# A two-block image kernel: statistics, projections and convolutions of the next image moved earlier, and the residual sum moved last in the chunk loop

## The chip, the cores and the metric

The kernel runs on one core of one Trainium2 chip. The metric is device time in microseconds (us), from the first to the last instruction of one launch, as the median of several runs. Engines: PE does matrix products, DVE (VectorE) and POOL (GpSimd) elementwise work, ACT (ScalarE) table functions and copies out of PSUM, SP issues the DMAs. Each works through its own list of instructions in order; semaphores tie them together.

## The reference, cut to what matters

`x` is (16, 192, 32, 32) in float32: 16 images of 192 channels and 1024 positions. Each image goes through two residual blocks, one after the other:

```python
def _L0_conv_ref(u, ...):                       # first block
    zxbcdt = useq @ in_proj_w.T                 # 192 -> 844 columns: z 384, xBC 448, dt 12
    dt = softplus(zxbcdt[..., -12:] + dt_bias)
    xBC = silu(depthwise_conv3x3(xBC) + conv_b) # over the 32x32 image
    x, Bm, Cm = split(xBC)                      # 384, 32, 32
    y = _chunk_scan(x, dt, A, Bm, Cm) + D * x   # 8 chunks of 128 positions, 12 heads
    y = layernorm(y) * norm_w + norm_b
    return (y * z) @ out_proj_w.T
def _L1_conv_ref(x, ...):                       # second block
    x_in, delta, Bm, Cm = split(seq @ W_proj.T + b_proj)
    delta = softplus(delta + dt_bias)
    y = _selective_scan(x_in, delta, A, Bm, Cm, D)   # 192 channels x 16 states, 1024 steps
    return y @ W_out.T + b_out
x = x + _L0_conv_ref(_gn(x), ...)               # _gn: 32 groups of 6 channels
x = x + _L1_conv_ref(_gn(x), ...)
```

## The kernel before

The work is a chain of passes. Pass b runs the second block's scan of image b beside the whole first block of image b+1; the first pass (b = -1) has no scan, the last two finish image 15. A pass is cut into 48 steps (`SLOTS`, the `s` in `run` of each engine), and every engine runs through the same steps in its own list. The order is fixed by hand, by a table of step numbers (`FILL_AT`, `CONV_AT`, `IM_AT`, `SSD_AT`, `P1_AT`) and by the order of the calls in each `run`. An engine that waits at one instruction holds up all that stands behind it in its list.

**The scan (image b).** One unit per step, 48 in all: ACT makes the decay factors (`decay`, L955), DVE multiplies the input (`inputs`, L1234) and runs the scan of the unit before (`scan_unit`, L1247), POOL multiplies by C (`states_by_c`, L754), and PE adds two units' states every second step (`sum_states`, the matmuls `bank<-hc,sel`). The unit's operands come by DMA from DRAM rows that the pass before wrote (`durep`, `bcrep`; `reads`, `keep`, `keep_rows`). The other half of `delta` gets its softplus on DVE in steps 1 and 2 (`softplus_piece`). Image b-1 gets its last output products in steps 10 to 13 (`finish`).

**The first block (image b+1).** In this order:
- step 0: channel statistics of the loaded image on DVE (`BATCH_NORM_STATS2 st<-xa`), step 1: their sums over groups on PE (`group_means`), step 2: `group_deviation` on DVE and `group_variances` on PE, step 3: `group_variance`, then POOL's power (`group_rstd`), step 4: the normalised image `xna`, `xnb` (`normalise_groups`, L1064 and L1065)
- steps 4 to 7: nine projection pieces on PE, "fills" (`fill`, `bank<-xna,wt0a`), copied by ACT one step later into `stage`, `bcst` and `dtx`
- steps 8 to 12: SP copies `stage` shifted by a pixel into `im` and `imb` (`shifted_copies`, 8 DMAs per convolution, L589)
- steps 8 to 11: four convolutions on PE (`conv`, `bank<-ssd,wcv`), three for x and one for B and C. ACT copies the three from PSUM into `xs` with the bias (`copy_conv`, L798), one step later
- steps 13 and 19: `silu` on ACT: Silu over both halves of `xs` (L892), and in step 13 over B and C from PSUM (L898). Each of the two loads the Silu table first and the exponential table afterwards
- steps 14 to 37: the chunk loop. Chunk c begins in step 14 + 2c; its parts stand 0 to 9 steps behind that (`chunk_at(s, stage)`). Two consecutive steps hold one part each of up to five chunks. In the second of the two steps DVE does, in order: the residual sum x1 = x + out of chunk c-4 (`residual`, L1125), the state carried on of chunk c-1 (`carry_state`, L1080 to L1083), the layer norm (L1112), the gate (L1119), and then the scan unit. PE's product `bank<-state,cs_` waits for the carried state
- from step 37 (`PRE_AT`): the statistics of x1, its `xna` at step 41, and the second block's eight projection tiles on PE (`project`, `bank<-xna,wt1a`): six at steps 41 to 47, the last two in steps 0 and 1 of the next pass. Then softplus and u for the first quarter (steps 43, 44), which SP writes to DRAM for the scan.

Program lines that the rows name: L798 `copy_conv`, L831 `exp_rows`, L892 `silu`, L1044 the channel statistics, L1053 to L1056 `group_deviation`, L1064 `normalise_groups`, L1082 `carry_state`, L1125 `residual`, L1234 `inputs`, L1284 PE's `mm`, used by nearly all products.

## Time and profile before

| | us |
|---|---|
| median of 3 runs | 4015.21 |
| lowest, highest | 3992.51, 4017.95 |
| profiled execution, its own time | 3989.59 |
| its span, first to last instruction | 3987.8 |

The profile is of one execution. A stretch of a pass is best read in the view of windows, which gives for each stretch the busy time of each engine and PE's granted clock as a share of full speed; the timeline then shows what an engine did there, and in brackets how long it had been idle and on what.

### The profile page before, as it was taken

What the parts mean: (1) busy time and instruction counts of PE and PEld (TensorE: products, weight loads), DVE (VectorE), ACT (ScalarE), POOL (GpSimd) and SP (SyncE); (2) the same over time, 40 slices, a digit from 0 to 9 for tenths busy, and PEclk for the clock granted to TensorE, in tenths of its full rate; (3) what the DMA queues carried; (4) which work ended last, traced back from release to release, by engine and by line L of the source; (5) the groups of instructions that cost most, each with busy time, mean ns of one, the idle gap of its engine ahead of it and who ended that gap; (6) DMA issues with size and microseconds to landing.
All of it is one profiled execution on the core that took longest, in us unless ns stands there. A gap on an engine that the chain in (4) does not pass through costs nothing. (4 is left out here: it accounts for less than half of the span.)

```text
span 3987.8 us, 62307 instructions
## 1 busy us (share of the span) xinstructions
PE 3274.6 (82%) x20256; PEld 1864.8 (47%) x20256; DVE 2674.3 (67%) x3855; ACT 1844.2 (46%) x4475; POOL 2035.9 (51%) x1363
## 2 busy tenths in 40 slices
PE   4778888887987978888887897978888888888875
PEld 2645446363453635436363463635536354463620
DVE  1346857678585776757678575775757668575798
ACT  1425454363544536444463534535454353544542
POOL 1325546364453745546365463745546364563755
PEclk8989989898998989989898998989989898998986
DMA  3032131312213132130422213132131312313122
GB/s 64 1 94 68 68 86 34 112 62 79 81 40 112 51 107 74 67 82 33 120 62 78 81 40 112 51 106 69 48 108 33 118 63 74 82 45 101 62 73 77
DMA packets 104179, 291.11 MB, mean 73 GB/s; under 512 B 25373, under 2 KB 27020, under 8 KB 103820
## 3 DMA queue, kind: packets, MB, share of 16 engines
q1 hardware_dynamic: 103820, 286.71, 23.8%
q8 instruction: 179, 2.93, 0.3%
q14 instruction: 180, 1.47, 0.1%
HBM read 181.84 MB, written 39.85 MB: 56 GB/s over the span
## 5 line engine op out<-in xcount | busy, mean ns | idle before, releaser
L754 POOL TENSOR_TENSOR hc<-hst,bcrep 128x512 f32<-128x512 f32 x768 | 1187.6, 1546 | 1227.8 <-DVE hst L1247 1199.8
L710 POOL TENSOR_TENSOR ssd<-ssd,cbt 128x512 f32<-128x512 f32 (+1 forms) x256 | 585.4, 2287 | 383.8 <-ACT ssd L831 364.2
L1234 DVE TENSOR_TENSOR wr<-durep,bcrep 128x512 f32<-128x512 f32 x768 | 644.4, 839 | 65.1 <-DMA bcrep<-bc_rows 65.1
L1284 PE MATMUL bank<-hc,sel 128*32 128x512 f32 x1536 | 474.6, 701 | 104.2 <-POOL hc L754 104.2
L955 ACT ACTIVATE bank<-durep,aneg 128x512 f32<-128x512 f32 x368 | 252.0, 690 | 514.0 <-DVE hst L1247 468.5
L831 ACT ACTIVATE ssd<-bank,ncs 128x128 f32<-128x128 f32 x1536 | 432.8, 401 | 74.6 <-PE bank L1284 72.5
L1284 PE MATMUL bank<-ssd 128*128 128x32 f32 (+1 forms) x3296 | 448.0, 288 | 7.4 <-POOL ssd L710 7.4
L1247 DVE TENSOR_TENSOR_SCAN hst<-dec,wr 128x512 f32<-128x512 f32 x256 | 358.2, 1399 | 135.6 <-ACT dec L955 63.0
L1284 PEld LDWEIGHTS bank<-ssd 128*128 128x128 f32 x3296 | 397.8, 193 | 15.1 <-POOL ssd L710 10.8
L1284 PE MATMUL bank<-xna,wt0a 128*128 128x128 f32 (+3 forms) x1088 | 320.1, 398 | 76.2 <-DVE xnb L1065 76.2
L861 ACT ACTIVATE ssd<-bank,nbc,nwc 128x128 f32<-128x128 f32 x384 | 147.8, 454 | 498.8 <-PE bank L1430 498.5
L1284 PE MATMUL bank<-ssd,wcv 64*32 64x512 f32 x5376 | 344.1, 591 | 0.0
L1247 DVE TENSOR_TENSOR_SCAN hst<-bank,carry,wr 128x512 f32<-128x512 f32 x240 | 306.9, 1279 | 29.4 <-issue 11.2
L955 ACT ACTIVATE dec<-durep,aneg 128x512 f32<-128x512 f32 x400 | 294.1, 740 | 7.1 <-DVE hst L1247 4.6
L1284 PE MATMUL bank<-xnb,wt0b 128*128 128x128 f32 (+3 forms) x1088 | 295.3, 374 | 0.0
L1284 PEld LDWEIGHTS bank<-xna,wt0a 128*128 128x128 f32 (+1 forms) x1088 | 183.1, 203 | 232.3 <-issue 195.5
L1368 PE MATMUL bank<-ident,csum 128*128 128x128 f32 x1536 | 257.3, 294 | 30.6 <-ACT ssd L831 30.6
L1368 PEld LDWEIGHTS bank<-ident,csum 128*128 128x128 f32 x1536 | 196.2, 149 | 89.4 <-ACT ssd L831 49.6
L1125 DVE TENSOR_TENSOR x1a<-bank,xa 128x128 f32<-128x128 f32 x128 | 37.1, 290 | 285.7 <-PE bank L1284 285.7
L1284 PEld LDWEIGHTS bank<-xnb,wt0b 128*128 128x128 f32 (+1 forms) x1088 | 178.7, 201 | 76.6 <-issue 76.6
L1247 DVE TENSOR_TENSOR_SCAN hst<-dec,carry,wr 128x512 f32<-128x512 f32 x144 | 209.2, 1453 | 6.9 <-issue 2.8
L1284 PE MATMUL bank<-ssd,wo 128*128 128x128 f32 (+1 forms) x1536 | 211.9, 280 | 1.2 <-DVE ssd L1119 1.0
(188 smaller groups left out, 5022.5 us busy)
## 6 DMA issues: line engine op xcount, KB each, us to landing
durep<-scratch SPq DMA_DIRECT2D x192, 512.0 KB, 3.8
bcrep<-bc_rows SPq DMA_DIRECT2D x128, 512.0 KB, 5.5
ssd<-stage SPq DMA_DIRECT2D x384, 140.4 KB, 2.9
ssd<-bcst SPq DMA_DIRECT2D x128, 74.4 KB, 2.1
xa<-in_x_dram SPq DMA_DIRECT2D x16, 512.0 KB, 5.3
scratch<-u SPq DMA_DIRECT2D x32, 256.0 KB, 2.0
scratch<-delta SPq DMA_DIRECT2D x32, 256.0 KB, 2.2
out_dram<-x1a SPq DMA_DIRECT2D x16, 512.0 KB, 5.1
```

Source lines behind the costliest of these rows:

```text
L710: nc.gpsimd.tensor_tensor(a, a, bc(cbt[:, c % 2, :].unsqueeze(1), [P, h1 - h0, Q]), ALU.mult).then_inc(att_ready.sem, 1)
L754: nc.gpsimd.tensor_tensor(hc[:, i % CRING, :], hst[:, i % HRING, :], bcrep[:, g, 1, :], ALU.mult).then_inc(hc_ready.sem, 1)
L831: ins = nc.scalar.activation(att[:, c % 2, h, :], bank[ROW_BANKS[r]][:, k * Q:(k + 1) * Q], ACT.Exp, bias=ncs[:, c, h:h + 1])
L861: ins = nc.scalar.activation(yzt[:, c % 2, m, :], bank[B_CBT][:, (m + 1) * Q:(m + 2) * Q], ACT.Identity, bias=nbc[:, m:m + 1], scale=nwc[: ...
L955: nc.scalar.activation(decay_of(i), durep[:, j % SLOTS_DU, 0, :], ACT.Exp, scale=aneg1[:, g * NB + k:g * NB + k + 1]).then_inc(decay_ready ...
L1125: nc.vector.tensor_tensor(x1a[par][:, t], bank[B_OUT][:, 0:Q], xa[:, t], ALU.add).then_inc(x1_ready.sem, 1)
L1234: nc.vector.tensor_tensor(wr[:, i % WRING, :], durep[:, j % SLOTS_DU, 1, :], bcrep[:, g, 0, :], ALU.mult).then_inc(w_made.sem, 1)
L1247: nc.vector.tensor_tensor_scan(hst[:, i % HRING, :], decay_of(i), wr[:, i % WRING, :], carry[:, g:g + 1] if hf else 0.0, ALU.mult, ALU.add ...
L1284: return nc.tensor.matmul(out, lhsT, rhs, start=start, stop=stop, skip_group_check=True)
L1368: nc.tensor.matmul(ps[:, k * Q:(k + 1) * Q], bc(csum[:, 0, c, h:h + 1], [P, P]), ident[:, :], start=(k == 0), stop=False, is_transpose=Tru ...
```

## The change

- **Statistics.** The statistics of image b+2 are taken in steps 42 to 46 of pass b (`EARLY_AT = 42`) instead of steps 0 to 3 of pass b+1; for image 0 they stand ahead of all passes. Their group sums go to bank 4, at other columns. `load_x` moves on SP from step 41 to step 38.
- **Projections.** `xna` is written in step 0, the fills stand in steps 0 to 2, their copies in steps 0 to 3. The chain of the step sizes dt moves with them, from steps 9 to 13 to steps 3 to 8.
- **Convolutions.** In the order x0, BC, x1, x2 at steps 3, 5, 7 and 10 instead of 8, 9, 10 and 11; the shifted copies at steps 2, 3, 4 and 7. `copy_conv` now puts each from PSUM through Silu with the bias and loads the exponential table again; `silu` is gone. `im` lies elsewhere in `ssd`, and the copies for x1 wait until the scan's softplus has left it.
- **Chunk loop.** It begins in step 13 instead of 14 (`SSD_AT`), with all that hangs on it. The residual sum stands last in its step on DVE, `layer_rstd` ahead of the second `attention` on POOL, and the exponentials of row block 1 ahead of the y copies on ACT.
- **Second block's projections.** All eight at steps 40 to 46 (`P1_AT`); none is left for the next pass.

The diff, cut to its core:

```diff
-FILL_AT = (4, 4, 5, 5, 6, 6, 6, 7, 7)
-CONV_ORDER = (0, 1, 3, 2)
-CONV_AT = (8, 9, 10, 11)
-IM_AT = (8, 9, 10, 12)
+FILL_AT = (0, 0, 1, 1, 1, 1, 2, 2, 2)
+FILL_COPY_AT = (0, 0, 1, 1, 2, 2, 2, 3, 3)
+CONV_ORDER = (0, 3, 1, 2)
+CONV_AT = (3, 5, 7, 10)
+IM_AT = (2, 3, 4, 7)
+IM_FILLS = (2, 6, 4, 9)
-SSD_AT = 14
+SSD_AT = 13
-P1_AT = (4, 4, 5, 8, 9, 10)
+P1_AT = (4, 4, 5, 7, 7, 8, 9, 10)
+EARLY_AT = 42
...
# SP, shifted_copies
+                sp.wait_ge(fill_copied.sem, fill_copied.at(n, IM_FILLS[u]))
+                if m == 1 and scan:
+                    sp.wait_ge(delta_ready.sem, delta_ready.at(n - 1, 3))
+                if m == 2:
+                    sp.wait_ge(conv_ps.sem, conv_ps.at(n, 1))
...
# ACT, copy_conv
+                for h in range(2):
+                    t = slice(h * HALF, (h + 1) * HALF)
+                    for q in range(2):
+                        if m < XM:
...
+                            ins = nc.scalar.activation(xs[m][r, t], bank[CONV_BANKS[u][q]][r0, :], ACT.Silu, bias=bias[r0, m:m + 1])
+                        else:
...
+                            ins = nc.scalar.activation((bs, cs_)[q][0:NS, t], bank[CONV_BANKS[u][h]][r, :], ACT.Silu,
+                                                       bias=cb[r, XM:XM + 1])
+                    ins.then_inc(conv_done.sem, 1)
+                nc.scalar.preload_act_table_set(EXP_LN)
...
# DVE, first_block_soon
-                if s == 4:
+                if s == 0:
                     if last:
                         dve.wait_ge(p1_ps.sem, p1_ps.at(n - 1, K_ALL))
                     normalise_groups(n, 0, xa[:, :], xb[:, :])
...
-                c = chunk_at(s, 9)
-                if c >= 0:
...
-                    residual(n, c, par)
...
# DVE, first_block_later (behind the scan unit and the inputs)
                 c = chunk_at(s, SSD_LAST)
+                if c >= 0:
...
+                    residual(n, c, par)
...
# DVE, run
+                    if more and s == EARLY_AT:
+                        loaded_stats(b + 2, early)
+                    if more and s == EARLY_AT + 2:
+                        group_deviation(b + 2, 0, early)
+                    if more and s == EARLY_AT + 3:
+                        group_variance(b + 2, 0)
...
# PE, start of the chunk loop
                     if c == 0:
-                        pe.wait_ge(silu_done.sem, silu_done.at(n, XM + 4))
                         pe.wait_ge(csum_ready.sem, csum_ready.at(n, 1))
-                        pe.wait_ge(conv_done.sem, conv_done.at(n, XM))
+                        pe.wait_ge(conv_done.sem, conv_done.at(n, 2 * len(CONV_ORDER)))
```

How the built program stands on the engines, at three places. PE, from the last steps of a pass into the next one (`mv` and `gq` are the image's statistics, `wt1a` and `wt1b` the second block's weights, `wt0a` the first block's). Before:

```order
L1284 MATMUL bank<-xna,wt1a 32x512
L1284 MATMUL bank<-xnb,wt1b 32x512
...
L1284 MATMUL bank<-mv,ga 128x1
...
L1284 MATMUL bank<-hc,sel 32x512 x2
...
L1284 MATMUL bank<-gq,ga 128x1
...
L1284 MATMUL bank<-xcm,diag1a 128x512
...
L1284 MATMUL bank<-hc,sel 32x512 x2
...
L1284 MATMUL bank<-xna,wt0a 128x512
```

And now:

```order
L1290 MATMUL bank<-mv,ga 128x1
...
L1290 MATMUL bank<-hc,sel 32x512 x2
L1290 MATMUL bank<-xna,wt1a 128x512
L1290 MATMUL bank<-xnb,wt1b 128x512
L1290 MATMUL bank<-gq,ga 128x1
...
L1290 MATMUL bank<-xna,wt1a 32x512
L1290 MATMUL bank<-xnb,wt1b 32x512
L414 UNCONDITIONAL_BRANCH
...
L1290 MATMUL bank<-hc,sel 32x512 x2
...
L1290 MATMUL bank<-xna,wt0a 128x512
```

The sums of the statistics now stand among the second block's projections, and a new pass (behind the branch) comes to its fills after one state sum.

ACT, around the last two convolutions (`dec<-durep` is the scan's decay). Before:

```order
L798 ACTIVATE xs<-bank,cb 64x512
L798 ACTIVATE xs<-bank,cbx 64x512 x2
L798 ACTIVATE xs<-bank,cb 64x512
...
L979 ACTIVATE x1b<-bank,boc 64x512
...
L892 ACT_TABLE_LOAD
L892 ACTIVATE xs<-xs 128x512 x3
...
L898 ACTIVATE bs<-bank,cb 32x512
L898 ACTIVATE cs_<-bank,cb 32x512
```

And now:

```order
L810 ACT_TABLE_LOAD
L810 ACTIVATE xs<-bank,cb 64x512
L810 ACTIVATE xs<-bank,cbx 64x512 x2
L810 ACTIVATE xs<-bank,cb 64x512
L816 ACT_TABLE_LOAD
...
L954 ACTIVATE dec<-durep,aneg 128x512
```

Each convolution has its own pair of table loads around its four instructions, and nothing of Silu is left behind the last one.

DVE, one step of the chunk loop. Before:

```order
L1125 TENSOR_TENSOR x1a<-bank,xa 128x128
L1126 TENSOR_TENSOR x1b<-bank,xb 64x128
L1082 TENSOR_TENSOR state<-state,cexp 32x384
L1083 TENSOR_TENSOR state<-state,bank 32x384
L1112 TENSOR_SCALAR ssd<-ssd,lmv,lrs 128x384
```

And now:

```order
L1079 TENSOR_TENSOR state<-state,cexp 32x384
L1080 TENSOR_TENSOR state<-state,bank 32x384
L1109 TENSOR_SCALAR ssd<-ssd,lmv,lrs 128x384
L1116 TENSOR_TENSOR ssd<-ssd,bank 128x384
L1241 SCALAR_TENSOR_TENSOR hst<-dec,carry,wr 128x512
L1228 TENSOR_TENSOR wr<-durep,bcrep 128x512
L1122 TENSOR_TENSOR x1a<-bank,xa 128x128
L1123 TENSOR_TENSOR x1b<-bank,xb 64x128
```

The carried state no longer stands behind the residual sum.

## Rows read from the trace of the kernel before

**Rows 1.** The page's part 1: busy us (share) and instructions per engine.

```profile
PE 3274.6 (82%) x20256; PEld 1864.8 (47%) x20256; DVE 2674.3 (67%) x3855; ACT 1844.2 (46%) x4475; POOL 2035.9 (51%) x1363
```

**Rows 2.** Windows of one pass: length; PE, PEld, DVE, ACT, POOL busy; PEclk, DMA, GB/s.

```profile
2411.90:2432.80 20.90, 9.35 (x26) 4.37 (x26) 19.85 (x30) 5.23 (x11) 7.94 (x6) 0.50 0.42 148
2432.80:2484.80 52.00, 51.90 (x452) 20.10 (x452) 21.81 (x30) 22.39 (x49) 14.46 (x9) 0.97 0.33 79
2484.80:2490.40 5.60, 0.07 (x3) 0.02 (x1) 3.29 (x4) 5.50 (x9) 3.17 (x2) 0.70 0.52 173
2490.40:2609.00 118.60, 106.02 (x701) 80.58 (x702) 90.20 (x136) 63.73 (x181) 80.15 (x53) 0.96 0.15 44
2609.00:2648.20 39.20, 33.86 (x86) 10.44 (x84) 32.14 (x44) 16.70 (x28) 20.41 (x14) 0.87 0.34 112
```

**Rows 3.** The instructions that write xna from the loaded image: durations in ns, first and last start in us.

```profile
L1064 DVE TENSOR_SCALAR xna<-xa,gm,gr x16: 812/1666/1668, 62.1 to 3628.8; 128x1024 f32<-128x1024 f32 x16
```

**Rows 4.** Timeline of PE, steps 1 to 4: start, us, instruction, [idle before <-releaser].

```profile
2415.30 0.59 PE L1284 MATMUL bank<-mv,ga 128*128 128x1 f32 x2 [6.51 <-DVE mv L1049]
...
2422.31 0.59 PE L1284 MATMUL bank<-gq,ga 128*128 128x1 f32 x2 [3.30 <-DVE gq L1056]
...
2432.84 2.04 PE L1284 MATMUL bank<-xna,wt0a 128*128 128x512 f32 x2 [4.90 <-DVE xnb L1065]
```

**Rows 5.** Timeline of PE, steps 8 to 14.

```profile
2451.67 1.05 PE L1284 MATMUL bank<-hc,sel 128*32 128x512 f32 x4
...
2452.97 5.38 PE L1284 MATMUL bank<-ssd,wcv 64*32 64x512 f32 x96
...
2466.06 5.36 PE L1284 MATMUL bank<-ssd,wcv 64*32 64x512 f32 x48
...
2490.39 0.79 PE L1284 MATMUL bank<-cs_,bs 128*128 128x128 f32 x2 [5.53 <-ACT cs_ L898]
```

**Rows 6.** Timeline of ACT, steps 9 to 13.

```profile
2459.15 1.38 ACT L798 ACTIVATE xs<-bank,cbx 64x512 f32<-64x512 f32 x2
...
2484.61 1.28 ACT L892 ACT_TABLE_LOAD   x1
2485.90 1.67 ACT L892 ACTIVATE xs<-xs 128x512 f32<-128x512 f32 x3
```

**Rows 7.** Timeline of PE, chunk loop, steps 23 to 25.

```profile
2552.55 0.91 PE L1284 MATMUL bank<-state,cs_ 128*128 128x384 f32 x2 [1.29 <-DVE state L1083]
...
2560.03 0.65 PE L1368 MATMUL bank<-ident,csum 128*128 128x128 f32 x4 [0.23 <-ACT ssd L831]
...
2566.20 0.91 PE L1284 MATMUL bank<-state,cs_ 128*128 128x384 f32 x2 [1.27 <-DVE state L1083]
```

**Rows 8.** Timeline of DVE, one step of the chunk loop.

```profile
2564.38 0.29 DVE L1125 TENSOR_TENSOR x1a<-bank,xa 128x128 f32<-128x128 f32 x1 [3.33 <-PE bank L1284]
...
2564.79 0.78 DVE L1082 TENSOR_TENSOR state<-state,cexp 32x384 f32<-32x384 f32 x1
```

**Rows 9.** Timeline of DVE, turn of the next pass.

```profile
2648.18 0.69 DVE L1234 TENSOR_TENSOR wr<-durep,bcrep 128x512 f32<-128x512 f32 x1 [3.16 <-DMA bcrep<-bc_rows]
2648.79 0.69 DVE L1044 BATCH_NORM_STATS2 st<-xa 128x6 f32<-128x512 f32 x1
...
2651.54 1.22 DVE L1247 TENSOR_TENSOR_SCAN hst<-bank,wr 128x512 f32<-128x512 f32 x1
...
2657.04 1.25 DVE L1054 TENSOR_TENSOR gd<-mv,gm 128x2 f32<-128x2 f32 x1
```

**Rows 10.** Timeline of SP, steps 8 and 9, and the copies' time to landing.

```profile
2438.65 11.45 SPq L589 DMA_DIRECT2D ssd<-stage  x16
...
DMA to landing us min/median/max: 2.3/2.9/4.1
```

**Rows 11.** Timeline of SP, last steps: u for the next scan goes to DRAM.

```profile
2637.99 0.34 SPq L521 DMA_DIRECT2D scratch<-u  x1
```

More of the change, by code:

```diff
@@ L755, in states_by_c, with run @@
                                         ALU.mult).then_inc(hc_ready.sem, 1)
-            def run(b, par, scan, end, first):
+            def run(b, par, scan, end, first, more):
                 for s in range(SLOTS if scan or first else 2):
@@ L767, in run @@
                         first_block(b + 1, s)
+                    if more and s == EARLY_AT + 4:
+                        group_rstd(b + 2, 0)
+            group_rstd(0, 0)
             passes(pool, run)
@@ L980, in finish, with run @@
                                          bias=boc[0:CB_, 1:2]).then_inc(out_ready.sem, 1)
-            def run(b, par, scan, end, first):
+            def run(b, par, scan, end, first, more):
                 step = Steps(act, act_steps, b + 1)
@@ L1248, in scan_unit, with run @@
                                              carry[:, g:g + 1] if hf else 0.0, ALU.mult, ALU.add).then_inc(scanned.sem, 1)
-            def run(b, par, scan, end, first):
+            early = Steps(dve, dve_early_steps, 0)
+            loaded_stats(0, early)
+            group_deviation(0, 0, early)
+            group_variance(0, 0)
+            def run(b, par, scan, end, first, more):
                 step = Steps(dve, dve_steps, b + 1)
+                early = Steps(dve, dve_early_steps, b + 2)
                 mid_step = Steps(dve, dve_mid_steps, b)
@@ L1579, in finish, with run @@
                     mm(o, wo1b[r, c], y1b[r, :], False, True).then_inc(o1_ps.sem, 1)
-            def run(b, par, scan, end, first):
+            def run(b, par, scan, end, first, more):
                 for s in range(SLOTS if scan or first else END_AT[1] + END_STEPS):
@@ L1618 @@
 PREPS = 15
-DVE_STEPS = 39
+DVE_STEPS = 35
+DVE_EARLY_STEPS = 4
 ACT_STEPS = 2
```

172 lines of the change are left out of this document (68 added, 104 removed).

## The prediction

> **What bounds the kernel now.** I began with the page's busy shares [rows 1]. No engine is full: PE is busy for 82% of the span, DVE for 67%. The bound must therefore change from stage to stage. The instruction that writes `xna` from a loaded image starts 16 times, first at 62.1 and last at 3628.8 us [rows 3]. One pass thus takes (3628.8 - 62.1) / 15 = 237.8 us. The windows cut one pass of 236.3 us into five stages [rows 2]:
>
> - Steps 0 to 4, 20.9 us: DVE is busy for 19.85, PE for 9.35 and only at half clock (1.2 of 2.4 GHz, share 0.50).
> - Fills and convolutions, 52.0 us: PE is busy for 51.9 of them, DVE for 21.8. PE bounds it.
> - Silu, 5.6 us: PE stands, ACT is busy for 5.5.
> - Chunk loop, 118.6 us: PE is busy for 106.0, DVE for 90.2.
> - Last steps, 39.2 us: PE busy for 33.9, DVE for 32.1. The scan units and softplus on DVE lead, PE follows closely.
>
> The timelines then name the gaps. In steps 1 to 4 PE waits three times for DVE's short statistics, 6.51, 3.30 and 4.90 us [rows 4]; behind the last comes the first fill. After the last convolution it waits 5.53 us for ACT's Silu [rows 5]. In the chunk loop it waits 1.27 us for the carried state and 0.23 us for ACT's exponentials in a chunk [rows 7]. The cause of the first stands on DVE [rows 8]: it sits 3.33 us in front of the residual sum, and the state (0.78 us and a second instruction) stands behind that in its list. PE had finished the state's product before.
>
> **The change, part by part.** All terms are per pass, against rows 2.
>
> *Steps 0 to 4.* The statistics leave, `xna` is written first. It takes 1.67 us [rows 3] and its `xnb` half of that: 2.5 us from its start to the first fill, in place of 20.9. The projections that PE did in these steps were already done while it waited. **-18.4 us.**
>
> *Fills and convolutions.* PE's work stays, and PE is full here. Added to the 52.0 us are what used to lie under the statistics: one state sum (1.05 us [rows 5]) and the product that opens the sum, 1.0 (half of the 2.04 of a pair of its size at half clock [rows 4]). The coupling is new: a convolution is 5.4 us of PE, the one for B and C too [rows 5]; ACT then needs two table loads of 1.28 and four instructions of 0.69 [rows 6], 5.35 us, and only behind them comes the decay for the next scan unit. That unit needs about 0.7 on ACT, 1.2 on DVE [rows 9] and 1.5 on POOL (the mean of all its instructions [rows 1]) before the sum on PE, so a state sum comes 9 to 10 us behind a convolution's end where it depends on it. It does so five steps behind the convolution. Between step 5 and step 10 PE has two sums, a small product and one convolution, 8.1 us, so it waits about 1.8 us. After step 3 it has over 13 us of other work, after step 7 over 12: hidden. The shifted copies take 11.45 / 16 = 0.72 us each to issue and 2.9 to land [rows 10], 8.6 us for the eight. Those for x0 can begin some 8 us after `xna`, and land at 17; the fills end at 21. The next eight land at 22 and 28, where PE wants them at 29 and 37. The DMAs stay hidden by 5 us or more. Together **+3.9 us**; bounds 0 (the coupling hidden) and +10 (each of the three earlier convolutions costs its 5.35 us of ACT, less what PE has to do meanwhile).
>
> *Silu.* The last convolution's copy is done 1.28 + 4 x 0.69 = 4.0 us after it. Before the chunk loop PE has in steps 11 to 13 five pairs of image b-1's output products of 1.0 us and a sum, over 6 us. They cover it. **-5.6 us**; if that cover were gone, 4.0 would come back.
>
> *Chunk loop.* With the residual sum last, DVE carries the state as soon as PE has made the product, over 2 us before PE asks for it. The wait of 1.27 goes in the four chunks in which a residual sum stands ahead, and that of 0.23 beside it with the new order on ACT: 4 x 1.5 = 6.0. A chunk now takes 2566.20 - 2552.55 = 13.7 us [rows 7], then 12.2, all of it PE's work; DVE is busy for 90.2 of 118.6 [rows 2], 10.4 of the 13.7. PE is late next, so no other engine takes the wait over. At the loop's start the pause for Silu is gone. The stage has a clock share of 0.96, so 0.08 of 118.6 us, 9.5, are at half clock, in which up to 4.7 are lost. The pause before it left the clock at 0.70. I take 3.5. The sums that DVE waits for in the last chunks cost up to 3.3 each [rows 8], mostly beside PE's own work: 2. One more state sum falls into the stage: +1.05. **-10.5 us**, bounds -4 (the state alone, little of it) and -14.
>
> *Last steps.* DVE gets four statistics instructions of 0.6 to 0.7 and the rest of them, 2.8 us, and the deviation (with one instruction of 1.25) 1.9 [rows 9]. A step more lies here, 1.22 + 0.69 [rows 9] = 1.9. Off goes the wait of 3.16 us for `bcrep` [rows 9]: from SP's first store of `u` [rows 11] to the end of that wait it is 10.2 us, and 13 us of steps and `xna` now cover it. The scan unit of 1.2 comes behind `xna`. The eight projections are now all ahead of `xna`. From the deviation on PE has its group sum, two projections and a state sum, about 6.0 us at full clock and 12 at half; DVE has three steps, 6.0. I take 2 of the 0 to 6. `load_x` is issued three steps earlier and has more than 10 us. **+4.2 us**, bounds +2 and +10.
>
> A pass: -18.4 + 3.9 - 5.6 - 10.5 + 4.2 = **-26.4 us**, 236.3 to 209.9. PE would be busy for over 90% of it. There are 15 such turns: 396 us. Image 0's first block, which runs without a scan, loses its own wait for Silu and those for the state, about 12. From the profiled execution's 3989.6 us: 3989.6 - 396 - 12 = 3582. That execution lies at the lower edge of the three timed runs, 0.6% below their median, so I round up to **3585**.
>
> A rule that speaks against this change is in the Trainium skill, "ScalarE: Activation LUTs", section "What ACT_TABLE_LOAD costs": every switch of tables costs a load of about 1.28 us and a drain of nearly 1.4 behind it, so functions should be grouped by table. This case's trace agrees with the load alone: the instruction behind it starts 1.29 us after the load's start [rows 6], so no drain shows. By the page's 2.66 us a convolution's copies would take 8.1 us instead of 5.35, and the sum would be some 4 us per pass less gain, 3645.
>
> **The rivals.**
>
> *The loads cost about double when they stand between matmuls' copies* (chance 0.07). Against it are the two loads of the row at 1.28 and their neighbours without a gap. Each copy would take 2 x 1.28 longer, of which PE has cover for the outer ones: 4.2 us per pass, 3582 + 63 = 3645.
>
> *ACT paces the convolutions* (0.14). For it: PE, ACT, DVE and POOL hand each scan unit on in order, and eight loads and 16 Silu instructions stand in eleven steps. If each of the three earlier convolutions costs PE 4 us of waiting, where I have 1.8 in all, and the last steps give back their upper bound (6 more), the gain is 26.4 - 10.2 - 4 = 12 us per pass: 3989.6 - 180 - 12 = 3798, and 3700 for half of it.
>
> *More than I count* (0.04): the clock stays up everywhere, the chunk loop reaches its bound: 32 us per pass, 3498.
>
> *No change* (0.02): the stages are only shifted, because a resource that I take as covered (the shifted copies, the scan's durations beside POOL) has no room: 3990.
>
> *Slower, through PE's clock in the last steps* (0.03). In steps 42 to 46 PE now waits for DVE between narrow group sums, the pattern before which it ran at 0.50 in steps 0 to 4 [rows 2, 4]. If it fell there and stayed, the 33.9 us of PE in this stage at share 0.87 would become 59, where DVE has 43.4: `xna` would be 15.6 us late, and the fills (18.8 us from 2432.84 to 2451.67 [rows 4, 5]) would take 16 more. That is 31.6 us against the 26.4 gained, +5.2 x 15: 4068. It decides once both together exceed 26.4 us. Against it: in the last steps the clock share was 0.87 with such group sums among them, and five of the eight projections keep PE busy around them.
>
> **The numbers.** The forecast has 0.70, with 3500 to 3690 from its bounds taken half together. The range must add the part of the coupling rival that lies below 3740 and the loads: **3490 to 3740** leaves out 0.17. A measurement of this kernel tells about 1% from no change. Faster by over 1%: all but the last two cases, **0.95**; within 1% **0.02**, slower **0.03**.
>
> **What would show it.** In the profile after: passes of about 210 us between the starts of `xna`; no PE wait on `mv` or `gq` above 2 us ahead of the fills and a first fill 2.5 us after `xna` starts; PE above 0.9 busy from there to the chunk loop; no PE wait for the Silu outputs; the wait on `state` gone for the later chunks; a chunk at 12.2 us; DVE's wait for `bcrep` gone; ACT_TABLE_LOAD at 1.28 with its neighbour at once behind it. It would be wrong if PE waits for POOL's `hc` by more than 3 us in steps 8 to 12, or if DVE waits for the eighth projection ahead of `xna` by more than 6.

## The result, and the profile after

The changed kernel takes 3692.76 us (median of 4 runs, 3677.62 to 3702.86), beside 4003.86 us for the kernel before on the same chip: a ratio of 0.9218, 95% interval 0.9163 to 0.9274. 3585 us had been forecast, in a range of 3490 to 3740. The gain is 311 us where about 420 were expected. The profile after is of the slowest of the four runs (3702.86 us) and the profile before of an execution below all its timed ones (3989.59 us). Two executions of the changed kernel differ by up to 25 us, 1.7 us a pass, so a stage's difference of that size between two profiles needn't come from the edit.

The page's part 1, busy times by engine, answers to [rows 1]:

```profile
PE 3197.5 (86%) x20256; PEld 1857.6 (50%) x20256; DVE 2943.3 (80%) x3855; ACT 1863.1 (50%) x4443; POOL 2115.8 (57%) x1363
```

The first surprise is here. VectorE (DVE) has the same 3855 instructions as before, and 269 us more of busy time. The instruction that opens a pass, with its shortest, median and longest duration in ns and its first and last start, answers to [rows 3]:

```profile
L1061 DVE TENSOR_SCALAR xna<-xa,gm,gr x16: 811/814/1420, 62.2 to 3346.2; 128x1024 f32<-128x1024 f32 x16
```

A pass takes (3346.2 - 62.2) / 15 = 218.9 us, for 237.8 before: 18.9 less, where 26.4 were forecast. The windows of one pass (busy PE, PEld, DVE, ACT, POOL, then PE's granted clock) answer to [rows 2]. They are: `xna` to the first fill, fills and convolutions, the way to the first `b_by_c`, the chunk loop, the last steps.

```profile
1573.40:1575.30 1.90, 0.00 (x0) 0.00 (x0) 1.90 (x3) 1.87 (x4) 0.52 (x1) 1.00 0.85 298
1575.30:1629.10 53.80, 51.06 (x445) 21.22 (x445) 33.58 (x42) 34.24 (x61) 20.18 (x13) 0.90 0.52 136
1629.10:1635.30 6.20, 6.14 (x19) 1.28 (x15) 4.02 (x5) 5.96 (x10) 3.25 (x2) 1.00 0.00 0
1635.30:1753.20 117.90, 104.24 (x706) 80.82 (x706) 111.65 (x141) 58.95 (x178) 88.28 (x55) 0.97 0.16 52
1753.20:1794.00 40.80, 32.91 (x102) 11.36 (x100) 34.93 (x54) 15.12 (x25) 18.69 (x14) 0.92 0.34 113
```

The chunk loop is as long as it was (117.9 for 118.6 us), but DVE is busy for 111.7 of it, where it was 90.2. Everywhere else the pass went much as planned. Means over the 14 passes from the second to the last but one, read from the starts of the named instructions, in us:

| stage | before | after | difference | forecast |
|---|---|---|---|---|
| last residual sum to the next pass's first fill | 61.03 | 43.64 | -17.4 | -18.4 + 4.2 = -14.2 |
| first fill to the end of the last convolution | 48.41 | 52.81 | +4.4 | +3.9 |
| from there to the first `b_by_c` | 11.17 | 5.93 | -5.2 | -5.6 |
| chunk loop | 118.85 | 119.28 | **+0.4** | **-10.5** |
| pass | 239.46 | 221.65 | -17.8 | -26.4 |

Inside the loop, the starts of PE's state products after the first `b_by_c` show where the chunks stand, again as means over these passes (the first chunk has none, so product 2 is the third chunk's):

| kernel | 1 | 2 | 3 | 4 | 5 | 6 | 7 |
|---|---|---|---|---|---|---|---|
| before | 10.3 | 22.3 | 34.2 | 47.9 | 61.5 | 75.2 | 89.0 |
| after | 9.4 | 21.9 | **37.6** | 50.3 | 63.0 | 75.8 | 89.2 |

The second product comes 0.4 us earlier and the third 3.4 us later, and the four that follow win only 3.2 us back. Product to product, they take 12.7 to 12.8 us (the last 13.4) where 12.2 were forecast and 13.7 measured before. So two things need a cause: the late third product, and the chunk of 12.7 to 12.8.

The timeline of DVE at the second product (start, duration, instruction):

```profile
1653.03 0.66 DVE L1228 TENSOR_TENSOR wr<-durep,bcrep 128x512 f32<-128x512 f32 x1
1653.61 2.69 DVE L1079 TENSOR_TENSOR state<-state,cexp 32x384 f32<-32x384 f32 x1
1656.34 0.54 DVE L1080 TENSOR_TENSOR state<-state,bank 32x384 f32<-32x384 f32 x1
```

The same on GpSimd (POOL), whose spans are rough:

```profile
1653.42 2.48 POOL L719 TENSOR_TENSOR ssd<-ssd,cbt 128x1024 f32<-128x1024 f32 x1
1655.85 1.58 POOL L761 TENSOR_TENSOR hc<-hst,bcrep 128x512 f32<-128x512 f32 x1
```

And on PE:

```profile
1652.08 1.05 PE L1290 MATMUL bank<-hc,sel 128*32 128x512 f32 x4
1657.03 0.94 PE L1290 MATMUL bank<-state,cs_ 128*128 128x384 f32 x2 [3.89 <-DVE state L1080]
```

The decay of the state is a product of 32x384 elements whose shortest length in this trace is 0.60 us. It began 0.2 us behind POOL's 2.48 us product and ended some 0.4 us behind its end: 2.69 us. PE stood for 3.89 us. Then its clock fell, as the two windows around the wait show:

```profile
1653.00:1657.00 4.00, 0.14 (x2) 0.00 (x1) 3.97 (x5) 1.75 (x5) 4.00 (x3) 1.00 0.03 11
1657.00:1661.00 4.00, 3.97 (x17) 3.51 (x18) 4.00 (x4) 1.14 (x4) 4.00 (x4) 0.59 0.02 4
```

PE is idle for 3.9 us of the first window, and in the second the granted clock is 0.59, mostly at the lower of its two levels (1.2 of 2.4 GHz). PE's work now runs right up to the loop, so the half-clock stretch that stood at its start before is gone, but another opens behind the second product. In the first 45 us of the loop PE is at half clock for 8.1 us of a pass before and for 9.0 after (means over the 14 passes, from the trace's records of the clock).

In the later chunks PE has another wait. Its timeline shows this one in a chunk of the changed kernel:

```profile
1703.21 0.46 PE L1290 MATMUL bank<-cs_,bs 128*128 128x128 f32 x2 [0.69 <-ACT ssd L880]
```

L880 is ACT's copy of the transposed output. Before the change, a state sum of the scan (`bank<-hc,sel`, 1.05 us) stood between the transposition and this `b_by_c` and covered the copy. The scan's sums stay in the even steps, and the loop now starts in an odd one, so the sum has come to stand ahead of the state product, and nothing covers the copy. From the third product to the seventh PE waits 2.74 us for this copy, 0.69 a chunk, and 0.49 for the state; before the change it was 5.01 for the state, 0.69 for the exponentials and nothing for the copy. These are the groups of the `b_by_c` over a whole run (count | busy, mean ns | idle before it, by what ended it), in the kernel before with the residual sum moved (kernel 1 below) and in the changed kernel:

```profile
L1283 PE MATMUL bank<-cs_,bs 128*128 128x128 f32 x256 | 68.1, 351 | 94.6 <-ACT cs_ L898 91.2 <-ACT ssd L861 3.4
L1290 PE MATMUL bank<-cs_,bs 128*128 128x128 f32 x256 | 57.5, 307 | 49.3 <-ACT ssd L880 44.5 <-ACT xs L810 4.7
```

The 91.2 us are the wait for Silu at the loop's start. L861 is the same copy in kernel 1: 3.4 us in a whole run, for 44.5.

DVE is nearly full in these chunks, busy for 48.4 of 51.6 us. Its timeline in one of them:

```profile
1704.53 2.78 DVE L1228 TENSOR_TENSOR wr<-durep,bcrep 128x512 f32<-128x512 f32 x1
1707.23 1.61 DVE L1079 TENSOR_TENSOR state<-state,cexp 32x384 f32<-32x384 f32 x1
```

Beside it on POOL:

```profile
1704.18 2.58 POOL L719 TENSOR_TENSOR ssd<-ssd,cbt 128x1024 f32<-128x1024 f32 x1 [0.43 <-ACT ssd L847]
1706.72 1.72 POOL L761 TENSOR_TENSOR hc<-hst,bcrep 128x512 f32<-128x512 f32 x1
```

`wr`, 0.66 us a moment ago, takes 2.78 behind the large product, and the state product then meets `hc`. The groups of the profile sort DVE's instructions in this kernel into two kinds. These work on SBUF alone and can stretch beside POOL: `wr` 0.65 to 2.79 us, the state product 0.60 to 2.71, the normalisation 0.46 to 2.52, the scan 1.20 to 2.92. The 128x384 products with an operand in PSUM stay at 0.53 to 0.56 us whether POOL works or not, the scans with one at 1.22 to 1.28, and `bn_stats`, with its one input, at 0.56. The Trainium skill, "SBUF — State Buffer", section "Who interferes with whom", states a rule for this: a VectorE instruction with two inputs in SBUF, beside a GpSimd one that reads SBUF, or one in a mode that uses both of VectorE's pairs of ports, needs a pair that GpSimd uses too; the pair is a lock for a whole instruction, and the one that is issued second stands. The trace agrees with its form: the state product ended 0.4 us behind POOL's, and wasn't slowed in proportion. Whether the normalisation, with one tensor in SBUF as input, runs in such a mode, no run here shows.

### The profile page after: what moved, and what is told of

The parts are those of the page before. It is cut to its first block and busy times, and to the rows that moved or that the text cites. A ratio compares the mean times of both kernels' runs of the same rounds, so it can differ in the third digit from the quotient of the medians.

```text
span 3701.1 us, 61373 instructions
## 1 busy us (share of the span) xinstructions
PE 3197.5 (86%) x20256; PEld 1857.6 (50%) x20256; DVE 2943.3 (80%) x3855; ACT 1863.1 (50%) x4443; POOL 2115.8 (57%) x1363
## 5 line engine op out<-in xcount | busy, mean ns | idle before, releaser
L761 POOL TENSOR_TENSOR hc<-hst,bcrep 128x512 f32<-128x512 f32 x768 | 1252.3, 1631 | 977.1 <-DVE hst L1241 938.7
L1228 DVE TENSOR_TENSOR wr<-durep,bcrep 128x512 f32<-128x512 f32 x768 | 769.6, 1002 | 1.4 <-DMA bcrep<-bc_rows 1.4
L1290 PE MATMUL bank<-hc,sel 128*32 128x512 f32 x1536 | 444.3, 663 | 122.5 <-POOL hc L761 120.7
L1241 DVE TENSOR_TENSOR_SCAN hst<-dec,wr 128x512 f32<-128x512 f32 x256 | 443.0, 1731 | 94.0 <-ACT carry L995 62.9
L1290 PE MATMUL bank<-ssd 128*128 128x32 f32 (+1 forms) x3296 | 467.4, 296 | 0.6 <-POOL ssd L719 0.4
L1290 PEld LDWEIGHTS bank<-ssd 128*128 128x128 f32 x3296 | 419.6, 202 | 5.6 <-POOL ssd L719 1.4
L1290 PE MATMUL bank<-xna,wt0a 128*128 128x128 f32 (+3 forms) x1088 | 305.8, 384 | 38.1 <-DVE xnb L1062 38.1
L880 ACT ACTIVATE ssd<-bank,nbc,nwc 128x128 f32<-128x128 f32 x384 | 147.5, 453 | 355.2 <-PE bank L1436 355.2
L1241 DVE TENSOR_TENSOR_SCAN hst<-bank,carry,wr 128x512 f32<-128x512 f32 x240 | 306.2, 1276 | 13.4 <-ACT bank L954 4.4
L1374 PE MATMUL bank<-ident,csum 128*128 128x128 f32 x1536 | 242.5, 282 | 11.5 <-ACT ssd L847 10.7
L724 POOL TENSOR_TENSOR lrs<-lve,neghalf 128x1 f32<-128x1 f32 x128 | 97.9, 765 | 241.2 <-DVE lve L1105 241.2
L1290 PEld LDWEIGHTS bank<-hc,sel 128*32 128x32 f32 x1536 | 58.8, 112 | 322.2 <-POOL hc L761 214.0
```

Source lines behind the costliest of these rows:

```text
L724: nc.gpsimd.tensor_tensor(lrs[:, c % 2:c % 2 + 1], lve[:, c % 2:c % 2 + 1], neghalf[:, 0:1], ALU.pow).then_inc(lrs_ready.sem, 1)
L761: nc.gpsimd.tensor_tensor(hc[:, i % CRING, :], hst[:, i % HRING, :], bcrep[:, g, 1, :], ALU.mult).then_inc(hc_ready.sem, 1)
L880: ins = nc.scalar.activation(yzt[:, c % 2, m, :], bank[B_CBT][:, (m + 1) * Q:(m + 2) * Q], ACT.Identity, bias=nbc[:, m:m + 1], scale=nwc[: ...
L1228: nc.vector.tensor_tensor(wr[:, i % WRING, :], durep[:, j % SLOTS_DU, 1, :], bcrep[:, g, 0, :], ALU.mult).then_inc(w_made.sem, 1)
L1241: nc.vector.tensor_tensor_scan(hst[:, i % HRING, :], decay_of(i), wr[:, i % WRING, :], carry[:, g:g + 1] if hf else 0.0, ALU.mult, ALU.add ...
L1290: return nc.tensor.matmul(out, lhsT, rhs, start=start, stop=stop, skip_group_check=True)
```

## The experiments

I went in with three theories for the missing 10.9 us of the chunk loop. **A**: DVE's idle time, once taken away, turns into longer instructions beside POOL. **B**: DVE comes late out of the convolutions. **C**: ACT's new order sets the chunk. **D**, that the odd first step of the loop makes the chunk longer, came with the seventh kernel. The ratios are to the kernel before, timed beside each, with 95% intervals.

**1. The residual sum last, and nothing else.** The four lines move from `first_block_soon` of the kernel before to its `first_block_later`:

```
-                c = chunk_at(s, 9)
-                if c >= 0:
-                    ...
-                    residual(n, c, par)
...
             def first_block_later(n, s, step, par, again):
...
                 c = chunk_at(s, SSD_LAST)
+                if c >= 0:
+                    ...
+                    residual(n, c, par)
```

> The kernel before, with one part of the change: the residual sum of a chunk is the last of its step on VectorE instead of the first; nothing else is moved. The prediction's working (residual out of the way, a chunk at the floor of the matrix work, 12.2 us) takes some 6 us off each of 15 passes: 4004 - 90 = 3915 us. Theory A (VectorE's and GpSimd's products slow one another down, so that VectorE's idle time in front of the residual turns into longer instructions of VectorE): chunks of 12.8 for 13.7 us at most, 3 to 4 us a pass, 3945 us, with the product wr going from 0.92 us to 1.2 or more in the chunk loop. Theory C (ScalarE's order sets the chunk): no change, 3990 to 4010 us.

Measured: 3900.48 us, ratio 0.9735 (0.9705 to 0.9765). From the third product to the seventh a chunk takes 12.1 to 12.6 us, the forecast's 12.2. So the step of the forecast was right for the kernel before, and theory A's 12.8 was wrong for it, though POOL's hold is there too: DVE is busy for 46.8 of the 49.2 us from the third product to the seventh, as full as after the change. DVE in a later chunk of this kernel:

```profile
1803.19 0.67 DVE L1233 TENSOR_TENSOR wr<-durep,bcrep 128x512 f32<-128x512 f32 x1
1803.88 2.61 DVE L1082 TENSOR_TENSOR state<-state,cexp 32x384 f32<-32x384 f32 x1
```

And POOL:

```profile
1803.39 2.69 POOL L710 TENSOR_TENSOR ssd<-ssd,cbt 128x1024 f32<-128x1024 f32 x1 [2.79 <-ACT ssd L831]
```

Here `wr` starts 0.2 us ahead of the product and escapes it; after the change it starts 0.35 us behind it and does not. One long stall a chunk here, a long and a middling one there. Neither makes PE wait long for the state: 0.39 us a chunk here, 0.16 there (the table behind kernel 9).

**2. The changed kernel with the residual sum first again** (the same lines moved back).

> The changed kernel with one part undone: the residual sum is again the first of its step on VectorE. Prediction's working and theory A: the idle time in front of the residual comes back (about 16 us over three chunks before), and the chunk goes from 12.8 to about 13.7 us: 3.6 us a pass, 3745 us. If the residual's place is worth nothing because VectorE and GpSimd share their work's time anyway, 3693 us, and wr falls back from 1.5 to 0.9 us in the later chunks.

Measured: 3709.80 us, ratio 0.9258 (0.9236 to 0.9280). The interval overlaps that of the whole change, and the medians' ratios differ by 0.4%. So the parts don't add up: alone, the residual's place is worth 2.7%. These are the groups of the residual's first instruction over a whole run, with DVE's idle time ahead of it. Before:

```profile
L1125 DVE TENSOR_TENSOR x1a<-bank,xa 128x128 f32<-128x128 f32 x128 | 37.1, 290 | 285.7 <-PE bank L1284 285.7
```

This experiment:

```profile
L1122 DVE TENSOR_TENSOR x1a<-bank,xa 128x128 f32<-128x128 f32 x128 | 36.8, 287 | 78.9 <-PE bank L1291 78.9
```

With the residual first, DVE still waits only 78.9 us for it, not 285.7: another edit had taken most of this wait away as well. And a chunk takes 12.7 to 12.8 us either way, with DVE busy for 44.8 us of four chunks instead of 48.4 and PE's 0.69 us for the copy as it was. What sets 12.8 is thus neither the residual nor a full DVE. My forecast of 13.7 failed here, and so did that of a short `wr` (its mean is 1.00 us in both kernels).

**3. ACT's copy of the scan's carry ahead of the convolutions' copies** (theory B).

```
 second_half(b, s, par, mid_step)
+if 2 <= s < HU + 2:
+    ...
+    nc.scalar.copy(carry[:, s - 2:s - 1], ...).then_inc(carried.sem, 1)
 ...
 first_block(b + 1, s, step, 1 - par, scan, end)
-if 2 <= s < HU + 2:
-    ...
```

> The changed kernel, with ScalarE's copy of the scan's carry put ahead of the first block's work in its step, so that it no longer stands behind the copy of a convolution (VectorE idles 5.00 and 2.37 us for it in the two steps before the chunk loop). Theory B (the loop loses its gain at its start, because VectorE comes late out of the convolutions): VectorE's 5.00 us wait goes, the state of the third chunk is there in time, its 3.9 us wait and the half-clock stretch behind it go; 4 to 5 us a pass, 3625 us. Theory A alone: VectorE starts two scans earlier, but its instructions stay stretched beside GpSimd's; 1 to 2 us a pass, 3670 us. If neither, 3693 us.

Measured: 3725.72 us, ratio 0.9318 (0.9289 to 0.9347), slower by 1.1%. DVE began the second product's decay of the state only 0.2 us earlier after the first `b_by_c`, and found the same POOL product in its way: 2.69 us again. So this edit hardly moved DVE and by itself says little on B. Kernel 8 below does: DVE begins the same decay no earlier there (18.7 us after the first `b_by_c`, for 18.5), and the loss is gone. B is out. The time is lost after the loop: from the last residual sum to the next first fill it takes 46.2 us for 43.6, with PE at half clock for 20.2 us of it for 13.2. Why was not tried.

**4 to 6. The two small orders undone.** In kernel 4 the copy of the transposed output stands ahead of the exponentials of the second row group again, in kernel 6 POOL's rstd behind its second attention product, in kernel 5 both.

```
 # ScalarE (4 and 5)
-c = chunk_at(s, 2)
-if c >= 0:
-    exp_rows(n, c, 1)
 c = chunk_at(s, 6)
 ...
+    exp_rows(n, c, 1)
     exp_rows(n, c, 2)
 # GpSimd (5 and 6)
-c = chunk_at(s, 4)
-if c >= 0:
-    layer_rstd(n, c)
 ...
     attention(n, c, HPB, NH)
+c = chunk_at(s, 4)
+if c >= 0:
+    layer_rstd(n, c)
```

In the expectation of kernel 4 I have this order the wrong way round: the edit puts the copy ahead of the exponentials, not behind them.

> The changed kernel with ScalarE's order undone: the copy of the transposed output stands behind the exponentials of the second row group again. Theory C (this order makes TensorE wait for the copy, 0.68 us a chunk, and so sets the 12.8 us): the wait changes and the pass with it; with the copy behind the exponentials (1.1 us) it should be there later and the wait should grow by about 1 us a chunk, some 5 us a pass, 3765 us. Theory A: TensorE is not the bound in the chunk loop, 3693 us within 15.

> The changed kernel with both small orders of the chunk loop undone: ScalarE's copy of the transposed output stands ahead of both later groups of exponentials again, GpSimd's rstd of the layer norm behind the second attention product again. Theory A, now in this form: a two-operand product, state product or normalisation of VectorE that lies in SBUF alone stands still while a GpSimd instruction runs (wr 2.79 us beside the 2.44 us product, 0.67 us free), so that the period of a chunk hangs on which VectorE instruction each GpSimd instruction meets. With the old orders GpSimd's 1024-wide product starts after wr, as in the kernel before with the residual last, and the chunk falls from 12.8 toward 12.2 us: 4 us a pass, 3635 us. If the two orders matter only through ScalarE's own time, 3732 us as with ScalarE's order alone undone. If the place of the chunk loop in the steps decides, 3693 us.

> The changed kernel with GpSimd's rstd of the layer norm behind the second attention product again, ScalarE's order as changed. Theory A: rstd comes 2.5 us later, so VectorE's normalisation waits for it, but wr may run before the product: between 3665 and 3720 us; the trace must show fewer long wr and the lost time as a wait for rstd or a longer state product. The rival that the chunk loop is bound by rstd's chain alone (stats, rstd, normalisation, transposition): 2.5 us a chunk, over 3900 us.

Measured: 4, 3732.33 us, ratio 0.9318 (0.9299 to 0.9336); 5, 3748.09, 0.9390 (0.9357 to 0.9423); 6, 3708.63, 0.9269 (0.9215 to 0.9322). Undoing ACT's order costs about 1%, 13.3 us a chunk for 12.8: the new order is worth keeping, and C, by which it did the harm, is wrong. Its wait is the right one, but the order on ACT doesn't make it: in 4 and 5 PE still waits 0.69 us a chunk for the copy, though ACT now does it first, and 0.48 more for the exponentials behind it. Undoing POOL's order makes no difference that can be told in 6; 5 lies 0.8% above 4 by the ratios, which come from two chips, and the chunk is 13.3 us in both. And A's forecast for 5, that the old orders would bring the chunk toward 12.2 us, failed too: `wr` did get short (0.86 us on average, for 1.00), and the chunk took 13.3 us. So the orders don't explain the difference between 12.2 and 12.8, and a long `wr` doesn't either.

**7. The loop from step 12 in place of 13**, the last five projections left in their steps.

```
-SSD_AT = 13
+SSD_AT = 12
-P1_AT = (4, 4, 5, 7, 7, 8, 9, 10)
+P1_AT = (4, 4, 5, 8, 8, 9, 10, 11)
```

> The changed kernel with the chunk loop starting at step 12 in place of 13 (as even as the 14 of before), and the last five projections left in their steps. TensorE then sums the scan's products in the same step of a chunk as before (between the transposed output and the next b_by_c) instead of beside the state product. Theory D (the odd start makes the chunk 12.8 us): 12.2 us a chunk, 0.6 x 7, 3630 us. Theory A: the period hangs on GpSimd's meetings with VectorE, which this shifts too, but the first chunks meet VectorE even less ready: 3640 to 3710 us. Theory B (VectorE late at the loop's start): one scan more is outstanding at the loop's start and the third chunk waits longer, 3710 us or more.

Measured: 3619.26 us, ratio 0.9067 (0.9033 to 0.9100): faster by 1.6%. The third product comes at 35.4 us instead of 37.6, later chunks take 12.5 us, and half clock in the first 45 us of the loop falls from 9.0 to 4.4 us. Theory B's price for it (3710 or more) was wrong, and A's (3640 to 3710) as well. D's 12.2 us was not reached either, though its total nearly was. But D names a true cause. With an even first step the state sum stands between the transposition and `b_by_c` again, and PE's wait of 0.69 us for the copy is gone. Another has taken most of its place: PE now waits 0.79 us a chunk for the state, for 0.16 before this edit.

**8. The large product of POOL in two halves.** The same multiplications, one instruction more per chunk:

```
-a = att[:, c % 2, h0:h1, :]
-nc.gpsimd.tensor_tensor(a, a, bc(cbt..., [P, h1 - h0, Q]), ALU.mult).then_inc(att_ready.sem, 1)
+for k in range(h0, h1, HPB):
+    a = att[:, c % 2, k:k + HPB, :]
+    ins = nc.gpsimd.tensor_tensor(a, a, bc(cbt..., [P, HPB, Q]), ALU.mult)
+ins.then_inc(att_ready.sem, 1)
```

> The changed kernel with GpSimd's 128x1024 attention product done as two of 128x512, the same work in two instructions. Theory A: VectorE's SBUF product stands still for one GpSimd instruction and gets its turn between two: the long wr (2.79 us) and the 2.69 us state product fall to about 1.9 us or less, and the chunk from 12.8 to 12.2 or 12.4 us: 3 to 4 us a pass, 3640 us. If the two engines only share the bandwidth evenly, the split changes nothing but GpSimd's own overhead: 3693 to 3700 us with wr as long as before.

Measured: 3597.80 us, ratio 0.9004 (0.8966 to 0.9042), 2.3% less than the change with no work taken away. The place of the second product, on DVE, POOL and PE:

```profile
1603.38 1.61 DVE L1080 TENSOR_TENSOR state<-state,cexp 32x384 f32<-32x384 f32 x1
```

```profile
1603.19 2.93 POOL L720 TENSOR_TENSOR ssd<-ssd,cbt 128x512 f32<-128x512 f32 x2
```

```profile
1605.71 0.88 PE L1291 MATMUL bank<-state,cs_ 128*128 128x384 f32 x2 [2.30 <-DVE state L1081]
```

The state product starts, as before, 0.2 us behind POOL's. It ends at 1604.99, in the middle of the 2.93 us that the halves take: it got its turn between them. PE waits 2.30 for 3.89 us. The window behind the wait, and the one ahead of it, have a granted clock of 1.00, where the changed kernel had 0.59:

```profile
1606.90:1610.90 4.00, 4.00 (x38) 3.97 (x36) 3.63 (x4) 1.14 (x4) 4.00 (x4) 1.00 0.01 2
```

Half clock in the first 45 us of the loop falls from 9.0 to 0.7 us a pass, and the third product comes at 32.5 us, 5.1 earlier. The shorter stall is 1.1 of this, and 8.3 us less at half clock are worth up to 4.2. That is theory A with a second link, at this one place: the hold makes one wait long, and the clock makes it expensive. It brought more than A's 3640 us. The later chunks are hardly shorter, though (12.5 to 12.6, where A had 12.2 to 12.4), and PE's wait of 0.68 us for the copy is still in each.

**9. Both, 7 and 8.**

> The changed kernel with the chunk loop from step 12 and the 128x1024 attention product in two halves, both gains together. Each alone took 5.5 and 6.8 us off a pass of 221.7. Theory A with the clock (the third chunk's late state product makes TensorE idle 3.9 us, and its clock falls to half for some 9 us of the loop): both remove that same stretch (4.4 and 0.7 us of half clock left), so they don't add up: 3570 to 3595 us. If the two were separate causes: 3692 - 15 x 12.3 = 3510 us.

Measured: 3597.82 us, ratio 0.8981 (0.8932 to 0.9030), the same as with the halves alone. The two gains don't add up, and the time is 3 us above the 3570 to 3595 expected, but the reason given there isn't what happened. The half-clock stretch isn't removed twice: it is partly back (5.6 us in the first 45 of the loop, for 0.7 in kernel 8), and the third product comes at 34.9 us instead of 32.5. The later chunks are at 11.7 us, below the 12.2 that I had called all PE's work, and the last steps take 2.2 us more (PE is at half clock for 16.1 us of them, for 12.5 in kernel 8). Why the clock falls at these two places again was not tried.

The chunk can now be laid beside PE's waits in it. These are means over the chunks between the third and the sixth product in the 14 passes, in us; PE does the same 86 matmuls in every one:

| kernel | first step of the loop | POOL's large product | chunk | wait for state | for ACT's copy | for exponentials |
|---|---|---|---|---|---|---|
| before | 14 | whole | 13.7 | 1.25 | 0 | 0.23 |
| 1 | 14 | whole | 12.2 | 0.39 | 0 | 0.22 |
| changed | 13 | whole | 12.7 | 0.16 | **0.69** | 0 |
| 5 | 13 | whole | 13.3 | 0.03 | **0.69** | 0.48 |
| 7 | 12 | whole | 12.5 | **0.79** | 0 | 0 |
| 8 | 13 | halves | 12.6 | 0.07 | **0.68** | 0 |
| 9 | 12 | halves | 11.7 | 0.07 | 0 | 0 |
| 12 | 12 | pieces | 11.7 | 0 | 0 | 0 |

The changed kernel and 7, 8 and 9 are all four cases of two edits. The even start takes the wait for the copy away, the halves that for the state. In the changed kernel the copy holds the later chunks, so the halves alone do little for them; once the start is even the state does, so the start alone does little; with both edits neither is left.

**10. No Silu, no loads of tables.** Leaves out the Silu on x, B and C.

```
-ins = nc.scalar.activation(..., ACT.Silu, bias=...)
+ins = nc.scalar.activation(..., ACT.Identity, bias=...)
-nc.scalar.preload_act_table_set(EXP_LN)
```

> The changed kernel without Silu: ScalarE's copies of the convolutions only add the bias, and the eight loads of tables in a pass (1.28 us each) are gone. Leaves out: Silu on the convolved x, B and C. The prediction put the price of this coupling at some 1.8 us in the convolutions' stretch and the loads otherwise beside TensorE's work. By it: convolutions' stretch 31.9 to about 30 us, and the way from the last convolution to the first b_by_c shorter by the one load ahead of the last copy, 1.3 us at most: 3 us a pass, 3645 us. Rival (the loads pace ScalarE, and through the carry copies VectorE, at the loop's start): VectorE is ready for the third chunk's state, the half-clock stretch goes as with the product in halves: 3570 to 3600 us.

Measured: 3688.65 us, ratio 0.9237 (0.9175 to 0.9300), no difference from the change. From the first convolution to the end of the last it takes 0.8 us less, from the first fill on 2.1 less. The last steps take 2.0 more, with PE at half clock for 19.5 us of them for 13.2. A pass is 0.9 us shorter in all: net, the eight loads of a pass, 10.3 us of ACT, cost about 1 us at most, and my 3 were too many.

**11. The halves in the kernel before.**

> The kernel before with one edit: GpSimd's 128x1024 attention product in two halves. Theory A: VectorE idles 29.6 us in the chunk loop of a pass there and its state product meets GpSimd's product seldom (0.95 us mean against 1.77 in the changed kernel), so the halves are worth little: 0 to 2 us a pass, 3970 to 3990 us. If the halves help in themselves (GpSimd's product reaching TensorE sooner), the same 6.8 us a pass as in the changed kernel: 3890 us.

Measured: 3961.27 us, ratio 0.9899 (0.9846 to 0.9953): 1.0%, for 2.3% in the changed kernel. With idle time on DVE the same hold costs less, but not nothing; my 0 to 2 us a pass were a little low (39 us in all, 2.6 a pass).

**12. Loop from step 12 and both products in pieces of 128x256.**

> The changed kernel with the loop from step 12 and both attention products of GpSimd cut into pieces of 128x256 (six instructions a chunk in place of two, the same work). Theory A (VectorE stands still for one GpSimd instruction): the stalls shrink to the length of a piece, some 0.6 us, wr to about 1.0 us; chunk 12.2 us: 3550 to 3580 us. If the pieces' own overhead on GpSimd weighs more (its share in the loop is about 80%), the chunk stays or grows: 3600 to 3640 us.

Measured: **3559.10 us**, ratio 0.8888 (0.8826 to 0.8950), the fastest of all, 3.6% under the change. The groups of the state product (count | busy, mean ns | idle), in the changed kernel and in this one:

```profile
L1079 DVE TENSOR_TENSOR state<-state,cexp 32x384 f32<-32x384 f32 x96 | 174.5, 1818 | 25.4 <-PE bank L1290 25.0
```

```profile
L1080 DVE TENSOR_TENSOR state<-state,cexp 32x384 f32<-32x384 f32 x96 | 93.4, 973 | 39.9 <-PE bank L1291 39.9
```

And those of `wr`, in the same order:

```profile
L1228 DVE TENSOR_TENSOR wr<-durep,bcrep 128x512 f32<-128x512 f32 x768 | 769.6, 1002 | 1.4 <-DMA bcrep<-bc_rows 1.4
```

```profile
L1229 DVE TENSOR_TENSOR wr<-durep,bcrep 128x512 f32<-128x512 f32 x768 | 645.1, 840 | 0.0
```

The stall follows the length of the piece: the state product's mean is 1.82 us beside a product of 2.56 us, 1.55 beside halves (kernel 8) and 0.97 beside pieces of 0.94. DVE's busy time is 2628.7 us, below the 2674.3 of before, while POOL pays 115 us more for the pieces. The later chunks take 11.7 us as in kernel 9, with no wait of PE left in them, so shorter stalls bring nothing more there. Of the 3.7 us a pass between the profiles of 9 and 12, 2.1 lie behind the loop, where PE is at half clock for 12.7 us in place of 16.1.

## Why the forecast held, and the step of it that failed

**Steps 0 to 4 and last steps, -14.2: right, 3.2 us too small.** In the two windows of one pass it is 1.9 us for 20.9, so -19.0 where -18.4 were forecast, and 40.8 for 39.2, so +1.6 where +4.2 were. The first fill starts 1.9 us after `xna`, which now takes 0.81 us in most passes where it took 1.67 [rows 3]. The waits on `mv` and `gq` moved to the last steps, where PE stands 1.5 and 2.3 us a pass for them, not 6.51 and 3.30 [rows 4]. DVE's wait for `bcrep`, 3.16 us a pass [rows 9], is 1.4 us in the whole run.

**Fills and convolutions, +3.9: right (+4.4).** The forecast put one coupling stall, about 1.8 us, at the state sum of step 10. PE's timeline of the pass has it there, of 2.70 us, and no other between the first fill and the end of the last convolution:

```profile
1621.59 1.05 PE L1290 MATMUL bank<-hc,sel 128*32 128x512 f32 x4 [2.70 <-POOL hc L761]
```

**Silu, -5.6: right (-5.2).** PE is busy for 6.14 of the 6.20 us ahead of the first `b_by_c`. The cover by the output products of the image before held.

**The loads of tables.** The rule of the Trainium skill, "ScalarE: Activation LUTs", section "What ACT_TABLE_LOAD costs", would have led to 3645 us by the prediction's working, but experiment 10 decides the case: without the loads the time is the same within the intervals. Nor does a drain show; the instruction behind a load starts 1.30 us after the load does:

```profile
1827.08 1.28 ACT L816 ACT_TABLE_LOAD   x1
1828.38 0.28 ACT L861 ACTIVATE dte<-dtx 128x96 f32<-128x96 f32 x1
```

**Chunk loop, -10.5: wrong, +0.4.** This is the step that failed, outside its own bounds of -4 and -14, and it failed in its reasoning: "PE is late next, so no other engine takes the wait over". In the kernel before that is so (kernel 1: a chunk of 12.2 us). In the changed kernel two other waits of PE took its place.

- *The later chunks, -6.0 forecast.* The wait for the state did go, from 1.25 to 0.16 us a chunk, but 3.2 us came, not 6.0. The 2.8 missing are about the 2.74 us that PE now waits for ACT's copy in these four chunks. The forecast counted "one more state sum" for the earlier start of the loop, at 1.05 us, and not that an odd first step takes the sum away from the place where it covered the copy. Nor was 12.2 us all PE's work: 11.7 is reached in kernels 9 and 12.
- *The clock at the loop's start, -3.5 forecast.* It did not come, as the half-clock stretch only moved behind the second product, where PE waits 3.89 us for a state product that stands behind POOL's. The third product comes 3.4 us later than before; with the halves (8) it comes 1.7 us earlier.
- *The sums of the last chunks, -2 forecast.* They were not seen: from the seventh product to the last residual sum it takes 29.9 us before and 30.1 after.

The forecast took DVE's 10.4 us in a chunk as a fixed amount. They are a figure with POOL often out of the way, because DVE spent 17.1 us of a pass idle ahead of its residual sums; with the idle time gone the same instructions took 111.7 us in the loop, not 90.2 [rows 2]. They still fitted into a chunk of 12.2 us in kernel 1. What cost time was one short product on PE's chain that met a long one of POOL, not the sum of DVE's work.

**What of this is shown, and what is not.** Shown: the stretch of SBUF-only instructions beside POOL, and its dependence on the length of POOL's instruction (8, 12); that it and the clock made the loss at the second and third product (8); that the odd start makes PE wait for the copy in the later chunks, and that behind it the wait for the state stood ready (7, 8 and 9 together). Shown too: the residual's place alone gives the forecast chunk of 12.2 us (1), and in the changed kernel almost nothing (2). Open: which of the other edits took DVE's wait for the residual away in kernel 2, and why PE's time at half clock in the last steps differs from kernel to kernel, from 12.5 us (8) to 20.7 (2).

**The range.** 3692.76 us lies between 3490 and 3740, but that is partly luck. It is above the forecast's own 3500 to 3690, in the part that was added for ACT pacing the convolutions. That did not happen: PE's one wait there is 2.70 us. The loss came from the chunk loop, of which the range expected a gain.

## What to carry to other kernels

Before you count an engine's busy share as room, ask which of its instructions share something with another engine, and whether its idle time is what kept them apart; taking a wait out of such an engine can return as longer instructions. Where a short instruction on the critical chain can meet a long one of GpSimd, cut the long one into pieces: the multiplications are the same, and halves gave 2.3% here. When a stage moves by a step against another, go through the engine that bounds it and see what stood ahead of each instruction that now waits: moving away a sum of 1.05 us that had covered a copy cost 0.69 us a chunk here. And before you call a theory dead because its edit did little, look at which wait PE has now: two waits can stand behind one another, and each edit alone then seems to be worth almost nothing. When a part of a change is worth 2.7% alone, don't add it to the others before you know that they don't remove the same wait.

## What the hardware showed that I had not expected

- After a PE wait of 3.89 us the next four microseconds ran at a clock share of 0.59, after one of 2.30 us at the same place at 1.00. With a stall on DVE that is 1.1 us shorter, the next state product came 5.1 us earlier, as the mean of 14 passes.
- The sequential scan on DVE is subject to the hold as well: 1.20 us at its shortest, up to 2.92 where POOL works beside it. With its decay in PSUM it stays at 1.22 to 1.28 us, in the same kernel.
- Cutting POOL's products has a price of its own, 327.6 + 259.7 us for 256 instructions against 699.8 us for 768, and the kernel was faster for it.
